# A two-layer graph network in fp32: VectorE's two head operations moved to the end of its stage, and the order of the two engines that read the head bank turned round

## The reference, cut to what matters

```python
msg_s, msg_v = (projected source row) + (projected destination row)
m1_s, m1_v = _cg_tp(msg_s, msg_v, y0, y1, rbf @ W_rbf ...)    # products, a dot and a cross with y1
a = leaky(m1_s @ W_alpha) * alpha_dot, summed per head        # logit of the softmax over a node's edges
val_s = m1_s @ Ws_val ; val_v = einsum(m1_v, Wv_val)
val_v = val_v * sigmoid(val_s @ Wg) ; val_s = sigmoid(val_s)
m2_s, m2_v = _cg_tp(val_s, val_v, y0, y1, w2_ss ...)
hs = m2_s @ Ws_vlin                                           # head scalars, 64 numbers an edge
hv = einsum(m2_v, Wv_vlin)                                    # head vectors, 32 x 3 numbers an edge
```

## Time and profile before

| | us |
|---|---|
| timed runs, median of 3 (lowest to highest) | 3868.43 (3867.98 to 3871.22) |
| the profiled execution, span | 4838.8 |
| of it the first layer (first to last L1610) | 140.2 to 3042.6 |
| DVE busy over the whole span | 3611.5 (75%) |
| PE busy | 3739.1 (77%) |
| ACT busy | 3088.6 (64%) |
| POOL busy | 2474.0 (51%) |

### The profile page before, as it was taken

One profiled execution on the slowest core, in us unless ns is written; L12 is line 12 of the kernel. 1 busy time (PEld: TensorE's weight loads), 2 busy tenths in 40 slices (PEclk: granted clock), 3 DMA queues, 4 the chain that ended last, 5 costly groups with the idle time before them and its releaser, 6 DMA issues. The chain is left out here.

```text
span 4838.8 us, 96593 instructions
## 1 busy us (share of the span) xinstructions
PE 3739.1 (77%) x21340; PEld 2828.7 (58%) x21340; DVE 3611.5 (75%) x12738; ACT 3088.6 (64%) x11217; POOL 2474.0 (51%) x2474
## 2 busy tenths in 40 slices
PE   3677777777777777777777778597788888888887
PEld 3676766666676767766666667487433333333334
DVE  4677777777777777777777778788677877777875
ACT  3566666666666666666666667475666666666664
POOL 3445555555555545555555454011366666666663
PEclk7899999999999999999999999799899998998998
DMA  3222222222222222222222222798233333333333
GB/s 101 64 64 68 72 67 68 67 70 67 66 71 72 67 63 72 68 72 67 66 68 68 64 71 63 228 274 226 60 77 77 77 79 76 79 78 77 81 78 103
DMA packets 296922, 411.02 MB, mean 85 GB/s; under 512 B 98580, under 2 KB 231572, under 8 KB 296596
## 3 DMA queue, kind: packets, MB, share of 16 engines
q0 software_dynamic: 127568, 211.04, 19.0%
q1 hardware_dynamic: 169284, 199.21, 12.7%
HBM read 309.09 MB, written 100.94 MB: 85 GB/s over the span
## 5 line engine op out<-in xcount | busy, mean ns | idle before, releaser
L654 POOL DMA_INDIRECT ACC<-src_tab,idx x784 | 777.2, 991 | 1184.8 <-DVE M L1532 852.2
L721 POOL DMA_INDIRECT ACC<-hid_tab,idx x784 | 828.7, 1057 | 453.6 <-issue 250.7
L800 PE MATMUL TR<-ident,M 128*128 128x128 f32 x4704 | 682.7, 285 | 472.0 <-DVE M L1532 380.3
L654 POOL DMA_INDIRECT TAB<-dst_tab,idx x784 | 767.9, 980 | 261.2 <-issue 260.9
L800 PEld LDWEIGHTS TR<-ident,M 128*128 128x128 f32 x4704 | 549.0, 146 | 554.6 <-DVE M L1532 440.0
L1126 ACT ACTIVATE MT<-TR 128x768 f32<-128x768 f32 x784 | 609.5, 842 | 158.2 <-remote 135.7
L1164 ACT ACTIVATE ACC<-HP 128x128 f32<-128x128 f32 x392 | 109.2, 279 | 750.8 <-DVE ACC L1619 625.8
L1115 ACT ACTIVATE ACC<-W,ACC 128x64 f32<-128x64 f32 x2352 | 587.9, 348 | 0.0
L849 PE MATMUL HP<-w_hv,MT 128*128 128x128 f32 x3136 | 564.4, 306 | 0.0
L1309 ACT ACTIVATE ACC<-TR,y 128x128 f32<-128x128 f32 (+1 forms) x1568 | 421.9, 455 | 208.6 <-remote 100.3
L1610 DVE TENSOR_TENSOR tG<-HP,ACC 128x192 f32<-128x192 f32 x392 | 140.1, 357 | 523.1 <-remote 331.3
(11 more groups left out here) (279 smaller groups left out, 8063.1 us busy)
## 6 DMA issues: line engine op xcount, KB each, us to landing
h_tab<-ACC SPq DMA_DIRECT2D x392, 160.0 KB
SC<-h_tab SPq DMA_DIRECT2D x50, 640.0 KB, 4.9
TAB<-h_tab SPq DMA_DIRECT2D x48, 640.0 KB, 5.1
ACC<-in_e64T SPq DMA_DIRECT2D x98, 256.0 KB
ACC<-src_tab,idx POOLq DMA_INDIRECT x784
TAB<-dst_tab,idx POOLq DMA_INDIRECT x784
ACC<-hid_tab,idx POOLq DMA_INDIRECT x784
agg_tab<-ACC POOLq DMA_DIRECT2D x49, 240.0 KB
```

The source lines that it names most:

```text
L654: pool.indirect_dma_start(tile[:, v.slot8, g, :], None, table.ap(), bass.IndirectOffsetOnAxis(ap=idx[:, v.sslot, c:c + 1], axis=0))\
L721: pool.indirect_dma_start(gat1[:, v.slot8, g, :], None, hid_tab.ap(), bass.IndirectOffsetOnAxis(ap=idx[:, v.sslot, c:c + 1], axis=0))\
L800: ins = nc.tensor.transpose(to[:, b * G + g, :], Mt[:, g, lo:lo + w], ident[:, :])
```

## The change

Three edits, all in the first layer. On ACT, `scalars0` waits for `h` (the head matmuls are done) in place of `hv` (VectorE has read the bank). On DVE, `head_products` waits for `hs` (ScalarE's copy is done) in place of `h`. And in DVE's stage `rest_of_v0` (L1531, L1532) comes ahead of `head_products`, so that the two head operations stand side by side at the stage's end. The number of instructions on each engine is the same.

```diff
@@ scalars0 (ACT)
-                act.wait_ge(LA["hv"], v.num + 1)
+                act.wait_ge(LA["h"], v.num + 1)
@@ head_products (DVE)
-                dve.wait_ge(LA["h"], v.num + 1)
+                dve.wait_ge(LA["hs"], v.num + 1)
@@ stage0 (DVE)
                 mixed_rest(t + -1, total, dots)
-                up = head_products(t + -2, total)
                 crosses = others0(t + 1, total, parts)
                 rest_of_s0(t + 1, total, parts)
+                rest_of_v0(t + 1, total, parts, crosses)
+                up = head_products(t + -2, total)
                 head_values(t + -2, total, up)
-                rest_of_v0(t + 1, total, parts, crosses)
```

## The result

The changed kernel takes 3938.15 us (median of 4 timed runs, 3937.43 to 3939.35), the kernel before 3868.2 (4 runs, 3866.71 to 3871.22). The ratio is 1.018, with a 95% interval of 1.0165 to 1.0194: 70 us slower. The forecast was 3942.

A forecast was written before the change was run, and what follows sets the result against it. VectorE (DVE) was taken to bound the kernel, with at most 256.9 us idle in timed runs. 3868 + 84 (dependent pair) - 10 (recovered waits) = 3942 us; range 3862 to 3965, slower at 0.80.

The forecast's parts named there:

- VectorE sets the pace: First layer: timed runs go at DVE's own pace, about 5.67 us a chunk, with nearly no waits on other engines.
- The budget: Whole kernel: timed median 3868.4 less DVE's busy 3611.5 leaves at most 256.9 us idle, so most traced waits cannot be real.
- The dependent pair: L1610 and L1619 on DVE, now neighbours: L1619 reads L1610's result, costing 0.215 us a chunk, 84 us in all.
- Recovered: DVE's real waits in the first layer that the change removes: 10 us taken, bounds 0 and 60.
- the turned wait on ACT: ACT's copy L1164 waits for `h` instead of `hv`, about 1.5 us earlier: worth 0 while DVE sets the pace.
- DVE's wait for `hs` costs 0: L1610 on DVE now follows ACT's copy, some 0.31 us later than the head matmuls: claimed hidden, cost 0.
- its margin: Before L1610: head matmuls may come 1.09 us later than before without delaying DVE (1.40 less 0.31).
- the cover: Six DVE operations, L1517 to L1532, run ahead of L1610 and hide ACT's copy: 1.40 us.
- the 122 that I gave as the price: At L1610, if the copy is not hidden: up to 0.31 us a chunk, 122 us.
- The profiled span would fall to 4570 to 4680: Whole profiled execution: a stage gains some 0.4 to 0.7 us, 160 to 270 us off the 4838.8 us span.
- the 1.77 us that I called unexplained: One traced stage before L1610: head matmuls end at 1512.47, L1610 starts at 1514.24, and no row explains the wait.
- L1543's wait: DVE's idle time before L1543 in the changed kernel's profile: expected above the earlier trace's 142.2 us.

The follow-up runs named there:

- e5_no_dependence: Changed kernel, but L1610 writes one of two buffers, L1619 reads the other, and the wait between them is removed (wrong product, timing only): 3854.67 us, ratio 0.9977.
- e4_values_apart: Changed kernel with L1531 and L1532 placed between the two head operations L1610 and L1619: 3856.58 us, ratio 0.9969.
- e1_before_again: The kernel before, unedited, profiled a second time: 3864.67 us, profiled span 3863.0 us.
- e2_order_only: Changed kernel with the old waits restored (ACT on `hv`, DVE on `h`), so only VectorE's new order is kept: 4118.4 us, ratio 1.0649.
- e6_values_gap_closed: Kernel before with L1512 moved between L1556 and L1574, and L1563 between L1574 and L1587: 3790.73 us, ratio 0.9814.
- e9_gap_closed_again: e6_values_gap_closed unchanged, run on another chip against the kernel before: 3797.47 us, ratio 0.9815.
- e3_waits_only: Kernel before with only the turned waits (ACT on `h`, DVE on `hs`), VectorE's order as before: 4145.75 us, ratio 1.0719.

## Why the prediction was right, point by point

**VectorE sets the pace: right, and it decided the sign.** The first profile read at face value, 523.1 us before L1610, called for a faster kernel. The budget (timed median less DVE's busy time, 256.9 us) said that those waits could not be in the timed runs. The second profile has 70.6 us of DVE idle time in the first layer (2198.4 - 2127.8) against 731.4 in the earlier trace rows. The layer runs at 5.62 us a chunk where I had worked out 5.67. The budget was 45 us short (301.9 us idle in the second profile): DVE is busy for 3561.1 us, not 3611.5, which was read from the long execution. Its parts were off both ways. The setup, the softmax stage and the end have 177.0 us of idle time where I kept 212.0, and the second layer has 54.3 where I had nearly nothing left.

**The dependent pair: right in kind, a little too large.** I took 0.215 us a chunk and 84 us from L1556 to L1574; it measures 0.187 and 73. The reason given, that the waits have the same form, does not hold: L1574 waits for three semaphores (`sg`, `m2a` and DVE's own), L1619 for two. Whether that makes the difference of 0.03 us no run shows. e5_no_dependence and e4_values_apart show that this gap and what hangs on it are the whole loss.

**A term I did not have: the jump back of the loop, 23 us.** The gap stands at the stage's end, and in each eighth stage the jump comes right behind it. The trace puts 17.7 of L1543's 18.1 idle us down to L1610. That DVE's sequencer used to run ahead of the operations and did the jump early, and now is held at the wait until L1610 has ended, is my reading and not shown; shown is that most of the idle time goes with the wait (2.8 us left in e5_no_dependence).

**Recovered: 10 taken, about 27 by the remainder above.** I had looked for it at L1610 and L1543. It was at L1506, 14.9 us in the second profile and as much, 14.2, in the earlier trace rows, since ACT's edge factors came late behind its wait for `hv`. All ten traces of normal length agree on this. In the four with the old wait (e1_before_again, e2_order_only, e6_values_gap_closed, e9_gap_closed_again) ACT's first operation behind its own jump, L1113, idles 46 times for 0.25 us, 11.4 us in all, and L1506 waits for ACT; in the six with the turned wait neither happens. I had called the turned wait on ACT worth 0. The two missed terms, +23 and -17, and the 11 too much for the pair, nearly cancel. That the sum came out 4 us from the measured time is luck; its sign and its largest term are not.

**DVE's wait for `hs` costs 0: right here (3.4 us at L1610), by its margin.** Where the cover is gone L1610 idles 247.5 us (e3_waits_only), twice the 122 that I gave as the price, because ACT, not the matmul, was late.

**The profiled span would fall to 4570 to 4680: wrong.** It is 3937.7. The step that failed took the long execution of the kernel before for what a profile does to this kernel. It was that one execution; neither a second profile of it nor any of the other eight kernels' shows it. What was late in it the trace does tell. The semaphore `h`, which says that the head matmuls are done, came after their recorded end by 1.4 us (median of the 370 that the trace recorded), in the second profile and in the changed kernel by 0.014. In the stage of the earlier trace rows it came at 1514.22, and L1610 started at 1514.24: that is the 1.77 us that I called unexplained. The granted clock of the first layer was 0.93, in the second profile 1.00. Why the matmuls or their signals were late stays open. For the same reason L1543's wait is 18.1 us, not above 142.2.

**The rules.** The Trainium skill ("VectorE: DVE Perf Modes", The DRAIN you can't avoid) has the next DVE operation start only on an empty pipeline, and reports for eight copies in a row that a semaphore after each costs nothing extra. Here it does cost: starts 0.27 us apart without the dependence and 0.45 with it, for the same two operations, and the measurement decides. The same section adds that a next operation that is not held starts earlier, which I had passed over; the 0.27 us between operations of 0.35 us agree with that. The Trainium skill ("Perfetto Trace Analysis", Per-instruction lifecycle) says that matmul ends in a profile are estimated. The long execution bears that out, with `h` 1.4 us behind the recorded ends; in the second profile, 0.014 us behind, the estimate was good.

## What to carry to other kernels

Hold each profile against the timed runs first: timed time less the busiest engine's busy time is about all the idle time that can be real (256.9 us by the long profile, 301.9 in the second), and a long wait that doesn't fit into it is no promise of a gain. On the engine that sets the pace, put independent work between an operation and the one that reads its result. Closing one such gap of the kernel before was worth 71 us here, and the turned waits with the copy moved ahead another 23, with no instruction less. When a wait is turned from one engine to another, look at what the other engine has queued ahead of the awaited operation.

## What the hardware showed that I had not expected

- A dependence between neighbours of 0.35 us on VectorE costs some 0.2 us between starts in both places seen here (L1556 to L1574: 0.48 against 0.27; L1610 to L1619: 0.45 against 0.27). Some 0.08 us of it do not show as idle time, because the lost overlap counts as busy.
- A loop's jump back on VectorE, hidden in the kernel before (L1543 0.27 us behind its forerunner in all stages but the last), costs 0.46 us a jump in the changed kernel, behind L1619's wait for L1610. In e4_values_apart and e5_no_dependence, where that wait does not hold, 0.12 to 0.13 us are left.
- One profiled execution of eleven was 25% longer than the timed runs and showed other bounds: 7.40 us a chunk for 5.62, and 523.1 us of waiting before one operation for 2.9.
